# The order of ScalarE's queue, a table for comparisons, and the first tile's softplus on VectorE, in a decoder layer of one core

## The chip, the cores and the metric

One core of a Trainium2 chip runs the whole program. The metric is the device time of one execution in microseconds; the median of three runs is given.

## The reference

A decoder layer on x of shape (4, 512, 512), float32. First a linear attention with 16 heads and decay, worked in chunks of 128 tokens, then an output projection, a residual sum and a layer norm. Then a state space model (selective scan) on a context of (4, 512, 256), gated by the rows of x:

```python
x = silu(xc + conv_b[None, :, None])                       # causal convolution of in_proj(ctx)
x_dbl = jnp.einsum('bdl,ed->bel', x, x_proj_w)
dt_low, Bm, Cm = jnp.split(x_dbl, [dt_rank, dt_rank + d_state], axis=1)
dt = jax.nn.softplus(jnp.einsum('brl,dr->bdl', dt_low, dt_proj_w) + dt_proj_b[None, :, None])
def step(state, inp):                                      # over 512 time steps
    dA = jnp.exp(d[..., None] * A)
    state = state * dA + (d * u)[..., None] * b[:, None, :]
    y = jnp.einsum('bdn,bn->bd', state, c)
y = (y + D[None, :, None] * x) * silu(z)
```

Residual and layer norm again; then a mixture of 64 experts, of which each token takes the 8 with the highest probability (at most 256 tokens an expert), and a last residual and layer norm.

## The kernel before

The program has two parts. `mixers` computes attention, state space model and routing for the four batches; `experts` runs the 64 experts behind it. The change is in `mixers` alone.

`mixers` gives each engine its own queue, written out by hand; semaphores tie them together. All queues follow one pattern: a loop over the batches b, in it the tiles c = 0 to 3 (128 channels of the scan, and at the same time a chunk of 128 tokens of attention, number t = 4b + c), and in it 8 steps k. A step n = 32b + 8c + k works two groups of states: ScalarE makes the decays (`decays`, L856, writes `hst`), GpSimd the inputs (`inputs`, L1120, writes `dbu`; it may run one step ahead), VectorE scans twice and multiplies with C (`scan`, L1301 and L1307), TensorE sums over the states (`sum_states`, L416). Between the steps stands the rest: TensorE's projections (q, k, v at L454, the output at L523), scores (L475), the turning of q and k; ScalarE's copies out of the PSUM ring of three banks (`take`, L831); GpSimd's rotation of q and k (L1193 to L1197), its roots (L1148, L1150) and, in batches 1 to 3, the scattering of the slot table (L1227); VectorE's masks on the scores (L1354), layer norm sums and routing. At tile c = 2 the next batch's convolution is made (`front`), at c = 3 its projections to B, C and the step sizes (`soft`).

The softplus of a tile m of a batch is spread over engines. ScalarE computes |x|, relu(x), exp(-|x|), 1 + it, a rounded copy and the logarithm (`soften`, `exponentials`, `rounded`, `logs`). Then GpSimd and ScalarE work in turn: `soft_parts` (GpSimd, L1126, L1127), `excess` (ScalarE, Relu, L902), `soft_rest` (GpSimd, L1132), `steps` (ScalarE, Relu, L906), `steps_of_u` (GpSimd, L1138, the product with u), which signals `dtu_ready`. SP's queue then copies the result 32 times into `rep` (`copy_steps`, L734), and only then can the decays and inputs of that tile be made. Tiles 0 and 1 are EARLY, tiles 2 and 3 LATE. Batch 0's tile 0 alone is done by VectorE in a row (`first_steps`, L1336 to L1348), before the loop. For tile 0 of batches 1 to 3 the turn is in c = 3 of the batch before: `soft_parts` at k = 4 and `soft_rest` and `steps_of_u` at k = 5 of GpSimd's loop. For tiles 1, 2 and 3 it is in c = 0 and 1 of their own batch. `soft_ready` counts the `soft_rest`s.

In c = 0 ScalarE's queue behind step 5's decays reads: the small copy of ssq, the copy of the k projection, `steps(b, 1)`, `exponentials(b, LATE)`, decays of step 6, and so on; near its end `excess(b, 2)`, decays of step 8, `excess(b, 3)`, the copies of qT and kT.

The routing of the third batch is turned into slots by comparisons: `number_slots` (in the last batch, c = 1, k = 7) computes places, and `make_hots` (L1472) compares them with 0 to 127, twice for each of four chunks of tokens, at the (c, k) of `HOT_AT`. They read `count16`, 128 values of 16 bits, broadcast along the last axis. For the last batch the same is done in the tail behind the loops, with `count8`, in which each value stands 8 times in a row, filled by L1625 in the tail.

## Time and profile before

| | |
|---|---|
| median of 3 runs | 1326.41 us (1325.27 to 1327.13) |
| the profiled execution | 1329.2 us, its span 1327.4 us |
| mean granted TensorE clock | 0.887 of full |
| VectorE busy | 1117.1 us, 84% |
| TensorE busy | 1140.0 us, 86% |
| GpSimd busy | 968.9 us, 73% |
| ScalarE busy | 847.4 us, 64% |

A timeline lists one engine's instructions by start. An idle time ahead of an instruction stands in brackets with the instruction that ended it; without brackets it followed the one before. Instructions in a row of the same line are drawn together (x2). The end of one and the start of the next may overlap by some 0.1 us.

### The profile page before, as it was taken

To read this page: it belongs to the slowest core of one execution; us is meant where nothing else is said; L and a number is where in the kernel's file an instruction comes from. 1 tells how busy PE (TensorE), PEld (TensorE's weight loads), DVE (VectorE), ACT (ScalarE), POOL (GpSimd) and SP (SyncE) were. 2 spreads that over 40 slices of the span, in tenths; PEclk is the share of its full clock that TensorE was granted. 3 is DMA by queue.
4 is the path that set the end of the run, shared out by engine and by line. 5 is a ranking of instruction groups with operands and counts; after the bars stand their busy time and mean duration, and the time that the engine had idled before them with its cause. 6 is when DMAs were issued, how large, how long until landed. Compare 5 with 4: busy or idle time off the path is not lost. (4 is left out here: it accounts for less than half of the span.)

```text
span 1327.4 us, 19360 instructions
## 1 busy us (share of the span) xinstructions
PE 1140.0 (86%) x6421; PEld 759.0 (57%) x6421; DVE 1117.1 (84%) x1564; ACT 847.4 (64%) x1522; POOL 968.9 (73%) x760
## 2 busy tenths in 40 slices
PE   7779998799988989898785659999999999999950
PEld 2334434444433533345332449989999899998940
DVE  3679998889888899888999648988988888888947
...
GB/s 300 80 80 250 89 57 103 143 96 36 66 127 118 74 84 50 136 61 121 69 47 74 100 118 221 306 303 297 301 305 303 305 294 306 301 309 305 285 142 321
DMA packets 95138, 235.03 MB, mean 177 GB/s; under 512 B 18608, under 2 KB 18864, under 8 KB 94400
## 3 DMA queue, kind: packets, MB, share of 16 engines
...
## 5 line engine op out<-in xcount | busy, mean ns | idle before, releaser
L1301 DVE TENSOR_TENSOR_SCAN hst<-hst,dbu 128x512 f32<-128x512 f32 x256 | 299.1, 1214 | 48.4 <-POOL dbu L1120 35.6
L1120 POOL TENSOR_TENSOR dbu<-rep,bc 128x1024 f32<-128x1024 f32 x128 | 301.7, 2361 | 51.7 <-PE y_ps L416 18.5
L1774 POOL DMA_INDIRECT sum_rows<-ye,tokens x128 | 205.3, 1604 | 102.4 <-ACT ye L1850 81.3
L416 PE MATMUL y_ps<-dbu,cs 128*32 128x512 f32 x512 | 161.7, 716 | 73.1 <-DVE dbu L1307 55.3
L856 ACT ACTIVATE hst<-rep,small_sb 128x512 f32<-128x512 f32 x256 | 166.0, 684 | 65.8 <-DVE dbu L1307 61.5
L1766 POOL DMA_INDIRECT xe<-x_rows,tokens x128 | 151.3, 1182 | 74.5 <-issue 37.8
L454 PE MATMUL ring<-first_raw,xT 128*128 128x512 f32 x384 | 176.2, 603 | 2.7 <-ACT made L878 1.9
L1307 DVE TENSOR_TENSOR dbu<-hst,bc 128x1024 f32<-128x1024 f32 x128 | 156.8, 1225 | 4.4
L1816 PE MATMUL low<-xh,w1h 128*128 128x256 f32 x512 | 151.0, 295 | 0.0
L1816 PE MATMUL low<-xl,w1h 128*128 128x256 f32 x512 | 145.7, 285 | 0.0
L1816 PE MATMUL low<-xh,w1l 128*128 128x256 f32 x512 | 145.7, 285 | 0.0
L454 PEld LDWEIGHTS ring<-first_raw,xT 128*128 128x128 f32 x384 | 69.5, 190 | 98.3 <-issue 98.3
L1926 DVE TENSOR_TENSOR w1l<-first_raw,w1h 128x1024 fp32r<-128x1024 f32 (+1 forms) x128 | 117.0, 956 | 9.7 <-ACT w1h L1868 0.7
L1919 DVE TENSOR_TENSOR xl<-turn,xh 128x512 fp32r<-128x512 f32 x128 | 82.7, 687 | 33.1 <-ACT xh L1860 32.4
L1868 ACT ACTIVATE w1h<-first_raw 128x1024 fp32r<-128x1024 f32 (+1 forms) x128 | 101.0, 844 | 5.5 <-PEq L162 5.5
L416 PEld LDWEIGHTS y_ps<-dbu,cs 128*32 128x32 f32 x512 | 20.9, 117 | 138.3 <-DVE dbu L1307 67.0
L1816 PEld LDWEIGHTS low<-xl,w1h 128*128 128x128 f32 x512 | 99.2, 194 | 0.0
L1816 PEld LDWEIGHTS low<-xh,w1h 128*128 128x128 f32 x512 | 99.0, 193 | 0.1
L1816 PEld LDWEIGHTS low<-xh,w1l 128*128 128x128 f32 x512 | 99.0, 193 | 0.0
L475 PEld LDWEIGHTS ring<-qT,kT 32*128 32x128 f32 x512 | 49.2, 280 | 61.0 <-ACT qT L831 28.3
L1804 PE MATMUL turn<-cs,xe 128*128 128x128 f32 x512 | 69.2, 279 | 13.6 <-DMA xe<-x_rows,tokens 12.7
L475 PE MATMUL ring<-qT,kT 32*128 32x128 f32 x512 | 57.3, 388 | 21.1 <-ACT kT L831 21.1
...
## 6 DMA issues: line engine op xcount, KB each, us to landing
first_raw<-in_gate_up SPq DMA_DIRECT2D x64, 768.0 KB, 9.9
rep<-made SPq DMA_DIRECT2D x256, 128.0 KB, 2.4
...
```

Of the source, the lines that this page charges most:

```text
L416: ins = pe.matmul(y_ps[rows, :], sel, dbu[:, n % WORK, g, :], start=(k == 0), stop=(k == QUADS - 1))
L454: ins = pe.matmul(ps[:, :], xT[:, t % 2, k, :], wqkv[:, "qkv".index(name), k, :], start=(k == 0), stop=(k == KD - 1))
L475: ins = pe.matmul(ps[:, g * P:(g + 1) * P], kT[r * HD:(r + 1) * HD, g, :], qT[r * HD:(r + 1) * HD, g, :], start=True, stop=True)
L856: act.activation(hst[:, at % HBANKS, :], rep[:, i % 2, g, 0, :], ACT.Exp, scale=a_sc[:, 4 * m + 2 * half + g, k:k + 1]).then_inc(da_ready, 1)
L1120: pool.tensor_tensor(dbu[:, n % WORK, :, :], rep[:, i % 2, :, 1, :], bc[:, k, 0, :].unsqueeze(1).broadcast_to([P, 2, T]), ALU.mult).then_i ...
L1301: dve.tensor_tensor_scan(h, h, dbu[:, n % WORK, i, :], 0.0, ALU.mult, ALU.add).then_inc(scanned, 1)
L1307: dve.tensor_tensor(dbu[:, n % WORK, :, :], hst[:, first:first + 2, :], bc[:, k, 1, :].unsqueeze(1).broadcast_to([P, 2, T]), ALU.mult).the ...
L1766: pool.indirect_dma_start(xe[:, e % RAW, j, :], None, x2_dram, bass.IndirectOffsetOnAxis(ap=tokens[:, e, j:j + 1], axis=0))\
L1774: pool.indirect_dma_start(sum_dram[e % SUMS], bass.IndirectOffsetOnAxis(ap=tokens[:, e, j:j + 1], axis=0), ye[:, e % YE, j, :], None, comp ...
L1816: ins = pe.matmul(dst, w[:, s, k, at:at + P], x[:, s, k, :], start=(k == 0 and n == 0), stop=(k == KD - 1 and n == 2))
L1868: act.activation(w1h[:, e % 2, :, cols], w1[:, e % RAW, :, cols], ACT.Copy).then_inc(w1h_ready, 1)
L1926: dve.tensor_tensor(w1l[:, e % 2, :, cols], w1[:, e % RAW, :, cols], w1h[:, e % 2, :, cols].bitcast(F32), ALU.subtract).then_inc(w1l_ready, 1)
```

## The change

Three things. On ScalarE, in c = 0, `steps(b, 1)` and `exponentials(b, LATE)` stand ahead of the copy of k, and `excess(b, 3)` behind the copies of qT and kT. The table `count8` lies in a tensor of its own, `counts`, whose first 16 rows hold the weights `dt_wT` until the last use; it is filled in `number_slots` at c = 1 of the last batch, and all comparisons read it (`count16` is gone). And `first_steps` now takes a batch: VectorE does tile 0's last five operations of the softplus in every batch, for batches 1 to 3 behind step 4 of c = 3; GpSimd's four and ScalarE's two operations for it are gone. `soft_ready` counts three a batch now.

```diff
--- before.py
+++ after.py
@@ -173,7 +173,8 @@
         wqkv = first_raw[:, :].rearrange("p (n k d) -> p n k d", n=3, k=KD)
         wo_sb = second_raw[:, 0:KD * D].rearrange("p (k d) -> p k d", k=KD)
         in_wT = second_raw[:, KD * D:].rearrange("p (k n) -> p k n", k=KC)
-        dt_wT = sb("dt_wT", [RANK, INNER])
+        counts = sb("counts", [P, INNER])
+        dt_wT = counts[0:RANK, :]
         small_sb = sb("small_sb", [P, S_END])
         xp_wT = small_sb[:, S_XP:S_R].rearrange("p (m r) -> p m r", m=MI)
         rT = small_sb[:, S_R:S_CONV].rearrange("p (k e) -> p k e", k=KD)
@@ -233,7 +234,6 @@
         tok_i = sb("tok_i", [P, TILES], I32)
         spill_f = sb("spill_f", [P, NT * TOPK])
         chosen = sb("chosen", [P, EXPERTS])
-        count16 = sb("count16", [P, P], F16)
         slot_i = sb("slot_i", [P, 3, NT, TOPK], I32)
         place_of = sb("place_of", [P, 2, NT, TOPK], F16)
@@ -257,7 +257,7 @@
         hot = acc[:, :, :].rearrange("p m t -> p (m t)").bitcast(F16).rearrange("p (i h s k) -> p i h s k", i=2, h=2, k=TOPK)
         hot_last = (bc[:, :, :, :].rearrange("p q a t -> p (q a t)").bitcast(F16)
                     .rearrange("p (j h s k) -> p j h s k", j=NT, h=2, k=TOPK))
-        count8 = xT[:, 0, :, :].rearrange("p k n -> p (k n)").bitcast(F16).rearrange("p (s k) -> p s k", k=TOPK)
+        count8 = counts[:, :].bitcast(F16).rearrange("p (s k) -> p s k", k=TOPK)
         tokens_f = tokens[:, :, :].bitcast(F32)
         tab_i, tab_f = u_sb[:, 2, 0:P].bitcast(I32), u_sb[:, 2, P:2 * P]
@@ -708,7 +708,7 @@
             def load_context(b):
                 if b:
-                    sp.wait_ge(soft_ready, MI * b - 1)
+                    sp.wait_ge(soft_ready, (MI - 1) * b)
                 sp.dma_start(ctxT[:, :, :], ctx_turned[b].rearrange("p (k t) -> p k t", k=KC)).then_inc(ctx_loaded, 16)
             def store_rows(b):
@@ -902,7 +902,7 @@
                 act.activation(ln[m], ln[m], ACT.Relu).then_inc(excess_ready, 1)
             def steps(b, m):
-                act.wait_ge(soft_ready, softened(b, m) - 1)
+                act.wait_ge(soft_ready, (MI - 1) * b + m)
                 act.activation(dt_of(m), dt_of(m), ACT.Relu).then_inc(dt_ready, 1)
             def take_mixed(t):
@@ -1049,27 +1049,24 @@
                         first_tap(b + 1, 2)
                     if soft:
                         rounded(b + 1, 1)
-                        excess(b + 1, 0)
                     if back and c == 1:
                         exponents(b - 1)
                     take_squares(t)
+                    if c == 0:
+                        steps(b, 1)
+                        exponentials(b, LATE)
                     if soft or (back and c == 1):
                         take(f"q{t + 1}", flat(qk[:, 0:HEADS, :]))
                     if more:
                         if c < NT - 1:
                             act.wait_ge(kdec_ready, (NT - 1) * b + c + 1)
                         take(f"k{t + 1}", flat(qk[:, HEADS:, :]))
-                    if c == 0:
-                        steps(b, 1)
-                        exponentials(b, LATE)
                     decays(n + 6)
                     for j in hots_due(n + 6, 2):
                         number_lows(j, hot[:, j % 2, 1, :, :])
                     if front:
                         first_tap(b + 1, 3)
-                    if soft:
-                        steps(b + 1, 0)
                     if c == 0:
                         rounded(b, 2)
                         logs(b, LATE)
@@ -1088,13 +1085,13 @@
                         decays(n + 8)
                         for j in hots_due(n + 8, 2):
                             number_lows(j, hot[:, j % 2, 1, :, :])
-                    if c == 0:
-                        excess(b, 3)
                     if more:
                         if c:
                             act.wait_ge(qdec_ready, (NT - 1) * b + c)
                         take(f"qT{t + 1}", flat(qT[:, :, :]))
                         take(f"kT{t + 1}", flat(kT[:, :, :]))
+                    if c == 0:
+                        excess(b, 3)
             first_norm(NT * B - 1)
             gate_z(B - 1, 3)
             for j in range(NT):
@@ -1266,14 +1263,8 @@
                             gate(b, k - 2)
                         if k == 2 and c == 3 and last:
                             gate(b, 2)
-                        if k == 4 and c == NT - 1 and not last:
-                            soft_parts(b + 1, 0)
-                        if k == 5 and c == NT - 1 and not last:
-                            soft_rest(b + 1, 0)
                         if k == 5:
                             mixed_root(t)
-                        if k == 5 and c == NT - 1 and not last:
-                            steps_of_u(b + 1, 0)
                         if k == (5 if c < NT - 1 else 6) and t + 1 < NT * B:
                             rotate(t + 1)
                         if k in (6, 7) and c == 0:
@@ -1330,22 +1321,23 @@
                     else:
                         ins.then_inc(drain_sem(use), 1)
-            def first_steps():
-                taken(dve, "dt0_0")
-                dve.wait_ge(soft_steps, 2)
+            def first_steps(b):
+                done, tile = 4 * MI * b, softened(b, 0)
+                taken(dve, f"dt{b}_0")
+                dve.wait_ge(soft_steps, done + (3 if b else 2))
                 dve.tensor_tensor(dt_of(0), dt_of(0), acc[:, 0, :], ALU.add).then_inc(part_steps, 1)
-                dve.wait_ge(soft_steps, 4)
-                dve.wait_ge(logged, 1)
+                dve.wait_ge(soft_steps, done + (7 if b else 4))
+                dve.wait_ge(logged, tile)
                 dve.tensor_tensor(ln[0], dtu_of(0), ln[0], ALU.subtract).then_inc(parts_ready, 1)
-                dve.wait_ge(part_steps, 1)
-                dve.wait_ge(parts_ready, 1)
+                dve.wait_ge(part_steps, tile)
+                dve.wait_ge(parts_ready, tile)
                 dve.scalar_tensor_tensor(out=dt_of(0), in0=ln[0], scalar=0.0, in1=dt_of(0), op0=ALU.max, op1=ALU.subtract)\
                     .then_inc(excess_ready, 1)
-                dve.wait_ge(excess_ready, 1)
+                dve.wait_ge(excess_ready, tile)
                 dve.tensor_scalar(dt_of(0), dt_of(0), -1.0, 0.0, ALU.mult, ALU.max).then_inc(dt_ready, 1)
-                dve.wait_ge(dt_ready, 1)
-                dve.wait_ge(u_ready, 1)
-                dve.tensor_tensor(dtu_of(0), dt_of(0), u_of(0, 0), ALU.mult).then_inc(dtu_ready, 1)
+                dve.wait_ge(dt_ready, tile)
+                dve.wait_ge(u_ready, MI * b + 1)
+                dve.tensor_tensor(dtu_of(0), dt_of(0), u_of(b, 0), ALU.mult).then_inc(dtu_ready, 1)
             def mask_scores(t, r):
                 use = f"s{r}_{t}"
@@ -1457,6 +1449,9 @@
                 assert own.n == ROUTE_STEPS, own.n
             def number_slots(b, own):
+                if b == B - 2:
+                    full(dve, f"dt{B - 1}_{MI - 1}")
+                    dve.tensor_copy(count8, cs[:, C_COUNT:C_COUNT + P].unsqueeze(2).broadcast_to([P, P, TOPK]))
                 own.settle()
                 own.step(dve.tensor_scalar(slot_i[:, 0, :, :], idxf[:, 0, :, :], float(P - 1), None, ALU.add))
                 own.settle()
@@ -1467,17 +1462,17 @@
                 dve.tensor_copy(place_of[:, 1, :, :], slot_i[:, 2, :, :]).then_inc(placed, 1)
                 assert own.n == PLACE_STEPS, own.n
-            def make_hots(j, hots, count):
+            def make_hots(j, hots):
                 for h in range(2):
                     ins = dve.tensor_tensor(hots[:, h, :, :], place_of[:, h, j, :].unsqueeze(1).broadcast_to([P, P, TOPK]),
-                                            count, ALU.is_equal)
+                                            count8, ALU.is_equal)
                 ins.then_inc(hots_made, 1)
             def number_tokens(j):
                 dve.wait_ge(placed, 1)
                 if j >= 2:
                     full(dve, f"slots{j - 2}")
-                make_hots(j, hot[:, j % 2], count16[:, :].unsqueeze(2).broadcast_to([P, P, TOPK]))
+                make_hots(j, hot[:, j % 2])
             def add_slots(use, done):
                 ps = full(dve, use)
@@ -1490,7 +1485,7 @@
                 own.settle()
                 dve.wait_ge(placed, 2)
                 for j in range(NT):
-                    make_hots(j, hot_last[:, j], count8)
+                    make_hots(j, hot_last[:, j])
                 taken(dve, "table")
                 ps = full(dve, "slots_last")
                 spares = key[:, 0:2, :].rearrange("p j e -> p (j e)").rearrange("p (e j) -> p e j", j=CJ)
@@ -1513,11 +1508,10 @@
                 convolve(0, m)
             dve.wait_ge(const_loaded, 16)
             dve.memset(ones16[:, :], 1.0)
-            dve.tensor_copy(count16[:, :], cs[:, C_COUNT:C_COUNT + P])
             dve.tensor_copy(below16[:, :], cs[:, C_TRI:C_TRI + P]).then_inc(halves_ready, 1)
             dve.tensor_copy(tok_i[:, :], cs[:, C_TOK:C_TOK + TILES])
             dve.tensor_copy(spill_f[:, :], cs[:, C_TRASH:C_TRASH + NT * TOPK])
-            first_steps()
+            first_steps(0)
             chain = {}
             for b in range(B):
                 last = b == B - 1
@@ -1575,6 +1569,8 @@
                         chain["norm"] = Chain(dve, norm2_steps, NORM2_STEPS * (b - 1))
                         second_sum(b - 1, chain["norm"], 0)
                         second_sum(b - 1, chain["norm"], 1)
+                    if c == NT - 1 and not last:
+                        first_steps(b + 1)
                     if back and c == 1:
                         choose(b - 1, chain["route"])
                     if front:
@@ -1622,7 +1618,6 @@
                 second_sum(B - 1, chain["norm"], j)
                 chain["norm"].settle()
                 dve.bn_aggr(mv2[:, j, :], st2[:, j, :]).then_inc(stats2_ready, 1)
-            dve.tensor_copy(count8, cs[:, C_COUNT:C_COUNT + P].unsqueeze(2).broadcast_to([P, P, TOPK]))
             chain["route"] = shift_logits(B - 1)
             choose(B - 1, chain["route"])
             find_slots(B - 1, chain["route"])
```

ScalarE in tile 0 of batch 0, behind step 5's decays, and at the tile's end (lines of the kernel before; L831 copies out of the ring, L906 is `steps`, L885 and L888 `exponentials`, L856 decays, L902 `excess`):

```order
@@ -47,8 +47,8 @@
 L856 ACTIVATE hst<-rep,small_sb 128x512 x2
 L914 ACTIVATE ssq<-ring0 128x1
-L831 ACTIVATE qk<-ring1 128x512
 L906 ACTIVATE made<-made 128x512
 L885 ACTIVATE acc<-acc 128x512 x2
 L888 ACTIVATE made<-acc,ones 128x512 x2
+L831 ACTIVATE qk<-ring1 128x512
 L856 ACTIVATE hst<-rep,small_sb 128x512 x2
```

```order
 L902 ACTIVATE ctxT<-ctxT 128x512
 L856 ACTIVATE hst<-rep,small_sb 128x512 x2
-L902 ACTIVATE ctxT<-ctxT 128x512
 L831 ACTIVATE qT<-ring1 128x512
 L831 ACTIVATE kT<-ring2 128x512
+L902 ACTIVATE ctxT<-ctxT 128x512
```

The copy of k has moved behind five instructions, and the second `excess` behind the copies of qT and kT.

GpSimd in c = 3 of batch 0, before (L1126, L1127, L1132 and L1138 are the softplus of the next batch's tile 0, L1120 the inputs, L1148 and L1150 the root):

```order
L1120 TENSOR_TENSOR dbu<-rep,bc 128x1024 x3
L1126 TENSOR_TENSOR made<-made,acc 128x512
L1127 TENSOR_TENSOR ctxT<-made,ctxT 128x512
L1120 TENSOR_TENSOR dbu<-rep,bc 128x1024
L1132 TENSOR_TENSOR made<-made,ctxT 128x512
L1148 TENSOR_SCALAR rms<-ssq 128x1
L1150 TENSOR_TENSOR rms<-rms,half_sb 128x1
L1138 TENSOR_TENSOR made<-made,u_sb 128x512
L1120 TENSOR_TENSOR dbu<-rep,bc 128x1024
```

and the same place after the change (its line numbers are three lower):

```order
L1117 TENSOR_TENSOR dbu<-rep,bc 128x1024 x4
L1145 TENSOR_SCALAR rms<-ssq 128x1
L1147 TENSOR_TENSOR rms<-rms,half_sb 128x1
L1117 TENSOR_TENSOR dbu<-rep,bc 128x1024
L1190 TENSOR_TENSOR rot<-qk,cs 128x512 x2
```

The four operations are gone; four input products follow one another.

VectorE after the change, at the same place (L1292 and L1298 are a step, L1328 to L1340 `first_steps`):

```order
L1292 SCALAR_TENSOR_TENSOR hst<-hst,dbu 128x512 x2
L1298 TENSOR_TENSOR dbu<-hst,bc 128x1024
L1328 TENSOR_TENSOR made<-made,acc 128x512
L1331 TENSOR_TENSOR ctxT<-made,ctxT 128x512
L1334 SCALAR_TENSOR_TENSOR made<-ctxT,made 128x512
L1337 TENSOR_SCALAR made<-made 128x512
L1340 TENSOR_TENSOR made<-made,u_sb 128x512
L1292 SCALAR_TENSOR_TENSOR hst<-hst,dbu 128x512 x2
L1298 TENSOR_TENSOR dbu<-hst,bc 128x1024
```

The five stand between step 4 and step 5; before the change the two steps followed each other there.

## Rows read from the trace of the kernel before

**Rows 1.** The page's part 1: busy us (share of the span) xinstructions.

```profile
PE 1140.0 (86%) x6421; PEld 759.0 (57%) x6421; DVE 1117.1 (84%) x1564; ACT 847.4 (64%) x1522; POOL 968.9 (73%) x760
```

**Rows 2.** Timeline of GpSimd: start us, us, engine, line, operation, tiles, count, [idle, releaser].

```profile
780.27 1.07 POOL L1766 DMA_INDIRECT xe<-x_rows,tokens  x1 [28.38 <-POOLq L162]
```

**Rows 3.** Timeline of VectorE, tile 0 of batch 0 and the start of tile 1.

```profile
74.21 2.35 DVE L1301 TENSOR_TENSOR_SCAN hst<-hst,dbu 128x512 f32<-128x512 f32 x2 [3.77 <-ACT hst L856]
...
84.59 2.35 DVE L1301 TENSOR_TENSOR_SCAN hst<-hst,dbu 128x512 f32<-128x512 f32 x2 [1.05 <-POOL dbu L1120]
...
90.81 1.29 DVE L1354 TENSOR_TENSOR pr<-ring,dmask 128x512 f32<-128x512 f32 x2 [1.96 <-PE ring L475]
...
92.02 2.33 DVE L1301 TENSOR_TENSOR_SCAN hst<-hst,dbu 128x512 f32<-128x512 f32 x2
```

**Rows 4.** Timeline of ScalarE, the same stretch.

```profile
70.16 0.60 ACT L831 ACTIVATE qk<-ring 128x512 f32<-128x512 f32 x1 [2.73 <-PE ring L454]
...
73.43 1.29 ACT L856 ACTIVATE hst<-rep,small_sb 128x512 f32<-128x512 f32 x2
...
87.03 0.63 ACT L902 ACTIVATE ctxT<-ctxT 128x512 f32<-128x512 f32 x1 [2.94 <-POOL ctxT L1127]
```

**Rows 5.** Timeline of TensorE, the same stretch: the k and the v projection.

```profile
66.38 3.68 PE L454 MATMUL ring<-first_raw,xT 128*128 128x512 f32 x8
...
75.59 3.70 PE L454 MATMUL ring<-first_raw,xT 128*128 128x512 f32 x8
```

**Rows 6.** Timeline of GpSimd, the same stretch: the product with u.

```profile
71.35 1.27 POOL L1138 TENSOR_TENSOR made<-made,u_sb 128x512 f32<-128x512 f32 x1 [3.31 <-ACT made L906]
```

**Rows 7.** Timelines of ScalarE, GpSimd and VectorE, tile 0 of batch 1.

```profile
231.75 0.60 ACT L831 ACTIVATE qk<-ring 128x512 f32<-128x512 f32 x1 [3.43 <-PE ring L454]
...
235.09 2.49 POOL L1193 TENSOR_TENSOR rot<-qk,cs 128x512 f32<-128x512 f32 x2
...
250.41 2.35 POOL L1120 TENSOR_TENSOR dbu<-rep,bc 128x1024 f32<-128x1024 f32 x1
...
253.61 2.33 DVE L1301 TENSOR_TENSOR_SCAN hst<-hst,dbu 128x512 f32<-128x512 f32 x2
```

**Rows 8.** Timeline of VectorE, second and fifth operation of `first_steps` in batch 0.

```profile
31.65 0.69 DVE L1339 TENSOR_TENSOR ctxT<-made,ctxT 128x512 f32<-128x512 f32 x1 [2.76 <-ACT ctxT L894]
...
33.64 0.69 DVE L1348 TENSOR_TENSOR made<-made,u_sb 128x512 f32<-128x512 f32 x1
```

**Rows 9.** Timelines of VectorE and GpSimd, boundary of batches 1 and 2.

```profile
362.83 2.35 DVE L1301 TENSOR_TENSOR_SCAN hst<-hst,dbu 128x512 f32<-128x512 f32 x2 [1.41 <-ACT hst L856]
...
379.03 2.35 DVE L1301 TENSOR_TENSOR_SCAN hst<-hst,dbu 128x512 f32<-128x512 f32 x2 [3.66 <-POOL dbu L1120]
...
362.73 2.35 POOL L1120 TENSOR_TENSOR dbu<-rep,bc 128x1024 f32<-128x1024 f32 x1
...
367.79 1.27 POOL L1138 TENSOR_TENSOR made<-made,u_sb 128x512 f32<-128x512 f32 x1 [0.54 <-ACT made L906]
```

**Rows 10.** Timelines of VectorE and GpSimd: L1415 beside GpSimd's product and in the tail.

```profile
626.79 3.01 DVE L1415 TENSOR_TENSOR x2T<-x2T,small 128x256 f32<-128x256 f32 x1
...
627.15 2.35 POOL L1120 TENSOR_TENSOR dbu<-rep,bc 128x1024 f32<-128x1024 f32 x1
...
760.77 0.42 DVE L1415 TENSOR_TENSOR x2T<-x2T,small 128x256 f32<-128x256 f32 x1
```

**Rows 11.** Line L1472: count, ns min/median/max; then the first eight with their busy us.

```profile
L1472 DVE TENSOR_TENSOR acc<-place_of,count x8: 1211/1800/5927, 657.7 to 721.4; 128x1024 f16<-128x1024 f16 x8
...
L1472 DVE TENSOR_TENSOR bc<-place_of,xT x8: 683/684/692, 768.0 to 772.2; 128x1024 f16<-128x1024 f16 x8
...
L1472 DVE TENSOR_TENSOR acc<-place_of,count 128x1024 f16<-128x1024 f16 x8 | 19.1, 2421 | 0.0
```

**Rows 12.** Timeline of VectorE in the tail: the table's filling.

```profile
750.18 0.66 DVE L1625 CAST xT<-cs 128x1024 f16<-128x1024 f32 x1
...
758.74 0.42 DVE L1404 TENSOR_REDUCE small<-ring 128x4 f32<-128x256 f32 x1 [7.90 <-PE ring L548]
```

2 lines of the change are left out of this document (1 added, 1 removed).

## The prediction

> **What bounds the kernel now.** I read the busy shares first. TensorE, VectorE and GpSimd are busy for 86, 84 and 73% of the span [rows 1], so the average names no limit and each stretch has to be read by itself. The execution falls in two parts. GpSimd issues the first gather of the experts at 780.27, having waited for the end of the first part (attention and state space model) [rows 2]. The change touches nothing behind that point, so all that is won or lost must be won or lost before it, and passes to the end one to one.
>
> In the first part VectorE runs 128 scan steps. Step n is two scans (2.33 us) and one product, some 3.5 us in all, with other VectorE work between. In the timeline of VectorE most steps start with no idle time before them, so the first part is VectorE's chain with holes, and the reader is to look at the holes in brackets. They stand at the same places in every batch: in tile 0 (chunk 0), at the start of tile 1, and at the first step of the next batch. In batch 0, step 6 waits 3.77 us for ScalarE's decays, step 8 1.05 for GpSimd's product, and the first mask of tile 1 1.96 for the scores of TensorE [rows 3]. The 1.96 before that mask and the 1.05 to 1.10 before step 8 are there in all four batches.
>
> ScalarE's timeline says why. It reaches the copy of the k projection at 67.4 and sits there until 70.16, because TensorE's projection ends only at 66.38 + 3.68 = 70.06; behind it in the queue stand one Relu, two exponentials and two additions (2.8 us), and behind those the decays of step 6 at 73.43 [rows 4, 5]. Later it waits 2.94 us for GpSimd's difference before the last `excess`, and the copies of qT and kT, which the scores need, stand behind that [rows 4]. GpSimd waits too: 3.31 us for the Relu [rows 6].
>
> **Part 1: the order on ScalarE in tile 0.** Nothing is added; three kinds of instruction change place. *Batch 0.* The Relu, exponentials and additions now run from 67.4 to 70.2, in the time that was spent waiting, and end when k is there. The k copy ends at 70.8. The decays of step 6 follow, so their first half is there at 71.4, and the step starts then instead of at 74.21: 2.8 us. GpSimd's product with u moves from 71.35 to 68.1 and the rotation behind it starts at 70.9 with the k copy, so everything behind that on GpSimd comes 2.6 us sooner, which is what steps 7 and 8 wait for. With qT and kT copied ahead of the last `excess` the 1.96 is gone as well. Step 8 starts at 84.59 - 2.6 = 82.0. Its two scans and its product take 3.5 us, the sum of tile 0's output and two masks 1.85, so step 9 starts at 87.35 instead of 92.02: **4.7 us**. What is behind the moved instructions: decays of step 9 now follow `excess`, whose operand is there at about 84.4, so they are ready by 85.7, in time. *Batches 1 to 3.* The same with a tighter bound. In batch 1 the rotation started at 235.09, and it can start behind the k copy at 231.75 + 0.60 = 232.35: 2.7 us [rows 7]. From there GpSimd has no idle time to the input product of step 9 of the batch, at 250.41 + 2.35 = 252.76, so those end at 250.1, and that is where the step starts that started at 253.61: 3.5 us [rows 7]. By the same two differences batch 2 gets 3.6 and batch 3 3.7. Sum of part 1: 4.7 + 3.5 + 3.6 + 3.7 = **15.5 us**. Tile 1 starts with TensorE, ScalarE and GpSimd all waiting for VectorE, so the whole pattern moves as one; TensorE has hardly any idle time in tile 2, but its unbroken run starts from VectorE's events and moves with them. Bounds: nothing beyond the first hole (2.8 + 3 x 1.1 = 6 us), if TensorE's projections hold the rest, and 15.5 + 2.
>
> **Part 2: the softplus of the first tile, at three batch boundaries.** Off GpSimd go four 128x512 operations a boundary (1.27 us each, as the last of them [rows 9], 5.1 us), off ScalarE two Relus; on VectorE come five. Where they stand today, in batch 0 with GpSimd idle, the last four take 33.64 + 0.69 - 31.65 = 2.68 us, and the first, which waited on its own there, is like the second, 0.69: 3.4 us [rows 8]. Take the boundary from batch 1 to 2. VectorE is through with step 4 at 362.83 - 1.41 = 361.4; step 5 starts at 362.83, step 0 of the next batch at 379.03 after a hole of 3.66, since the GpSimd chain gives its result at 367.79 + 1.27 = 369.06 and the copies of SP's queue follow it [rows 9]. Four of the five operations have both inputs in SBUF, and such an operation does not run beside one of GpSimd: with 3.01 us for what takes 0.42 in the tail, L1415 at 626.79 ended at 629.80, just behind the end of GpSimd's product at 627.15 + 2.35 = 629.50 [rows 10]. GpSimd, rid of its softplus work, starts its next product, that of step 6, some 1.9 us before 362.73, where it starts now, when TensorE's sum of step 3 is done, and holds to 363.2 [rows 9]. So the five end at 363.2 + 3.4 = 366.6, with GpSimd's two tiny roots between them 367.1. That is 2.0 us before 369.06, but step 5 now starts 4.3 us late, and steps 5, 6, the attention sum (1.7) and 7 at 3.5 us each put step 0 at 379.3 instead of 379.03: **+0.3**. The same working gives +0.7 at the first boundary and +0.2 at the third: **+1.2 us**. The five operations are hidden by the hole that the old chain left (1.41 + 3.66 us and a small one between), so this trade is nearly even. SP's copies start 2 us sooner, and its row loads behind them; inputs of step 1 of the next batch come 2.3 us sooner on GpSimd. I count none of it, because tile 0 is then held by the k projection, which follows VectorE. Bounds: without any waiting for GpSimd the five end at 364.8 and step 0 starts at 376.9, 2.1 us sooner (4.4 for the three boundaries, by the same working); for the upper end see the second rival.
>
> The Trainium skill ("SBUF — State Buffer", section on SBUF's two separate sides) states that VectorE operations with two SBUF inputs and GpSimd's operations hold one port pair by an exclusive lock, for the whole instruction. The trace agrees, with 3.01 against 0.42 us. By that rule at its worst this part costs what the second rival says; without it this part would give 4.4 us instead of costing 1.2.
>
> **Part 3: the comparisons and their table.** `make_hots` now reads a dense 16-bit table instead of one broadcast along the last axis. Of the eight in batch 3 the shortest took 1.21 us; the eight in the tail, which read such a dense table, 0.68 each [rows 11]. 8 x 0.53 = 4.2 us. The rest of the 19.1 us that they take is waiting for GpSimd: the longest of them lasted 5.93 us, beside two products of GpSimd in a row [rows 11]. I leave that waiting as it is. GpSimd's own small operations stand behind them in the same way, so its chain moves too. **-4.2 us**; ends 0 (the gain goes into new waits for GpSimd) and 19.1 - 4.9 = -14 (no waiting at all, as in the tail). The table's filling, 0.66 us, moves from the tail, where a wait of 7.90 us hides it [rows 12], to the end of tile 1 of batch 3, where VectorE is the chain: **+0.9** with a short wait for GpSimd (0.7 to 3). Removing it from the tail gives nothing. The small cast at the start stood under a wait too.
>
> **Sum.** -15.5 + 1.2 - 4.2 + 0.9 = -17.6. The profiled execution took 1329.2 us (span 1327.4), so it would take 1311.6; the median of the runs stands 2.8 lower, at 1326.4, and would become **1308.8**, say 1309.
>
> **Rivals.** *Half the gain stays behind TensorE* (0.18). The copies of k and v are then paced by TensorE alone. For it: the v projection (75.59 + 3.70) ends at 79.3, and v is taken before the decays of step 8 [rows 5]. Against it: step 8 is at 82.0 in my working, later than that. Part 1 would give 7.7, and the time 1316.6. *The lock turns the sign* (0.04). The place is the five operations at a boundary; if each of the four with two SBUF inputs meets a whole GpSimd product (2.36), a boundary costs 9.4 + 3.4, less the 5.3 of holes, 7.5 us; three are 22.5, and with -15.5 and -3.3 the time is 1330. It decides from 6.3 us a boundary. For it: the longest comparison sat through two products in a row [rows 11]. Against it: GpSimd's next product needs step 5's scan, so it has nothing long to run after 363.2. *The comparisons do not reach the dense rate in the middle* (0.08): no -4.2, 1313. *The comparisons also dodge GpSimd's products*: the 14 us of part 3 in place of 4.2, or half of them, 1299 to 1304 (0.12). The forecast itself has 0.55, with 1304 to 1314; 0.03 is left for no change, if the holes of tile 0 open again elsewhere.
>
> **Numbers.** A measurement of this kernel can tell 0.2%, 2.7 us. Faster 0.93, same 0.03, slower 0.04. The range that holds eight in ten runs from the dodging case to the TensorE case: 1302 to 1318.
>
> **What would show it.** After: no wait of ScalarE ahead of the four operations behind ssq in tile 0, holes before steps 6, 7 and 8 below 1 us and the mask's 1.96 gone; step 9 of batch 0 near 87.4; five VectorE operations in 4.5 to 6 us at each boundary, the first of them long; the hole of 3.66 gone, step 0 of batch 2 about as long after step 4 as before; comparisons in batch 3 with a minimum near 0.68; the first gather near 763. Wrong would be: tile 0 of batches 1 to 3 shorter by under 2 us, or the five operations over 8 us.

## The result and the profile after

| | before | changed |
|---|---|---|
| median beside one another | 1325.84 us (4 runs) | 1306.15 us (4 runs, 1304.74 to 1307.75) |
| ratio | | 0.9864, 95% interval 0.9827 to 0.9901 |
| the profiled execution | 1329.2, span 1327.4 | 1305.6, span 1303.8 |
| VectorE busy | 1117.1 | 1124.0 |
| mean granted TensorE clock | 0.887 | 0.900 |

The forecast was 1308.8, with 1302 to 1318. The changed kernel ran beside the old one twice more, in the experiments: 0.9899 (0.9884 to 0.9914) and 0.9872 (0.9844 to 0.9900). So the gain is 13 to 18 us; the 19.7 us between the two medians in the table are more than any of the three ratios gives.

The page's part 1, beside [rows 1], and the first gather of the experts in GpSimd's timeline, beside [rows 2]:

```profile
PE 1126.6 (86%) x6421; PEld 751.5 (58%) x6421; DVE 1124.0 (86%) x1578; ACT 844.8 (65%) x1516; POOL 954.8 (73%) x748
```

```profile
760.00 1.07 POOL L1761 DMA_INDIRECT xe<-x_rows,tokens  x1 [27.20 <-POOLq L162]
```

VectorE is busy for 7 us more and the program is shorter, because the work went into holes. The gather starts 20.3 us sooner. The experts, which the change leaves alone, took 547.1 us in the profile before and 543.8 here; other profiled executions with the same experts have 542.5 to 547, so this part is chance.

To see where the 20.3 us come from I set scan step against scan step: how much sooner each of the 128 starts than in the profile before.

| at the start of | batch 0 | batch 1 | batch 2 | batch 3 |
|---|---|---|---|---|
| step 0 | 1.6 | 4.7 | 8.7 | 11.9 |
| step 9 | 5.7 | 9.2 | 12.1 | 16.0 |
| step 12 | 4.2 | 6.9 | 11.3 | 15.2 |
| step 4 of c = 3 | 4.7 | 7.4 | 11.3 | 18.9 |
| step 5 of c = 3 (behind the five operations) | 0.3 | 4.7 | 7.0 | 18.8 |

Three things stand in it. Tile 0 gains 4.1, 4.5, 3.4 and 4.1 us by step 9 and gives 0.8 to 2.3 back by step 12. The five operations cost 4.3 us at once (2.7 in batch 1, where a wait of 1.41 had stood, [rows 9]), and all of it is back by the next step 0. Batch 3 gains 3.7 us more behind step 12, from the comparisons. And 1.6 us were there before any scan step. The lead is 18.7 us at step 127 and 20.3 at the gather; the stretch between them gained 0.0 to 1.6 us in every other profile too (1.4 in p1b_excess_only, which has nothing of parts 2 and 3), so these 1.5 us are not put down to any part.

**Tile 0.** VectorE's timeline, tile 0 of batch 0 and the start of tile 1, beside [rows 3]:

```profile
70.37 2.35 DVE L1292 TENSOR_TENSOR_SCAN hst<-hst,dbu 128x512 f32<-128x512 f32 x2 [2.69 <-ACT hst L856]
...
80.93 2.35 DVE L1292 TENSOR_TENSOR_SCAN hst<-hst,dbu 128x512 f32<-128x512 f32 x2 [1.18 <-POOL dbu L1117]
...
85.10 1.28 DVE L1346 TENSOR_TENSOR pr<-ring,dmask 128x512 f32<-128x512 f32 x2
86.30 2.33 DVE L1292 TENSOR_TENSOR_SCAN hst<-hst,dbu 128x512 f32<-128x512 f32 x2
...
97.33 2.35 DVE L1292 TENSOR_TENSOR_SCAN hst<-hst,dbu 128x512 f32<-128x512 f32 x2 [1.40 <-POOL dbu L1117]
```

The masks wait no more, and step 9 starts at 86.30. But step 6 still waits 2.69, and a hole that was not there before has opened at step 11: 1.40, for GpSimd. The timelines of ScalarE and of GpSimd in the same stretch, beside [rows 4, 6]:

```profile
69.09 0.60 ACT L831 ACTIVATE qk<-ring 128x512 f32<-128x512 f32 x1 [1.64 <-PE ring L454]
...
83.37 0.63 ACT L902 ACTIVATE ctxT<-ctxT 128x512 f32<-128x512 f32 x1 [1.20 <-POOL ctxT L1124]
```

```profile
69.82 2.49 POOL L1190 TENSOR_TENSOR rot<-qk,cs 128x512 f32<-128x512 f32 x2 [2.36 <-issue]
...
94.91 4.70 POOL L1117 TENSOR_TENSOR dbu<-rep,bc 128x1024 f32<-128x1024 f32 x2
```

The k copy waits for TensorE's projection as before, with the moved work behind it already done. GpSimd's rotation starts with it, and from there to the input product of step 11, the first of the pair at 94.91, GpSimd is never idle; that product ends at 97.3, where the step starts. When k is there depends on the clock too. The k projection on TensorE, first here, then in the third profile of the changed kernel (after_third), with step 6 in that profile:

```profile
63.61 5.38 PE L454 MATMUL ring<-first_raw,xT 128*128 128x512 f32 x8
```

```profile
67.29 3.68 PE L454 MATMUL ring<-first_raw,xT 128*128 128x512 f32 x8
...
72.43 2.35 DVE L1292 TENSOR_TENSOR_SCAN hst<-hst,dbu 128x512 f32<-128x512 f32 x2 [0.94 <-ACT hst L856]
```

The projection took 5.38 us here, at a mean granted clock of 0.68 of full, and 3.68 before [rows 5] and in after_third. With these instructions ahead of the copy, step 6 waits 2.69 us in all five profiles in which the projection took 5.38, and 0.94 to 1.00 in all four in which it took 3.68.

**The boundary.** Timelines of VectorE and GpSimd, batches 1 and 2, beside [rows 9]:

```profile
353.89 1.76 DVE L1328 TENSOR_TENSOR made<-made,acc 128x512 f32<-128x512 f32 x1
355.57 0.68 DVE L1331 TENSOR_TENSOR ctxT<-made,ctxT 128x512 f32<-128x512 f32 x1
...
357.55 0.69 DVE L1340 TENSOR_TENSOR made<-made,u_sb 128x512 f32<-128x512 f32 x1
358.16 2.34 DVE L1292 TENSOR_TENSOR_SCAN hst<-hst,dbu 128x512 f32<-128x512 f32 x2
...
370.29 2.34 DVE L1292 TENSOR_TENSOR_SCAN hst<-hst,dbu 128x512 f32<-128x512 f32 x2
```

```profile
352.75 2.35 POOL L1117 TENSOR_TENSOR dbu<-rep,bc 128x1024 f32<-128x1024 f32 x1 [1.31 <-DVE hst L1292]
355.67 0.63 POOL L1145 TENSOR_SCALAR rms<-ssq 128x1 f32<-128x1 f32 x1 [0.57 <-ACT ssq L914]
356.39 1.17 POOL L1147 TENSOR_TENSOR rms<-rms,half_sb 128x1 f32<-128x1 f32 x1
```

The first of the five lasts until GpSimd's product is through (352.75 + 2.35 = 355.10); the others run at 0.68 and 0.69 (0.43 for the one with a single input). In all 358.16 - 353.89 = 4.27 us, and 4.34 and 4.35 at the other two boundaries. How long the five take follows what is left of the product when they start: at this boundary the other profiles have 0.27 us left and 3.33 for the five (after_again), 0.97 and 4.03 (after_third), 1.94 and 5.00 (p2_first_tile), and here 1.21 and 4.27, each time 3.06 us more than what was left. GpSimd's tiny roots pay instead: 0.63 and 1.17 us, where they take 0.19 and 0.57 without a neighbour (as at 574.90 further down). Step 0 at 370.29 follows without a hole; the 3.66 is gone.

**The comparisons.** Line L1467 in VectorE's groups (busy, mean ns), beside [rows 11]:

```profile
L1467 DVE TENSOR_TENSOR acc<-place_of,counts 128x1024 f16<-128x1024 f16 x8 | 14.8, 1889 | 0.0
L1467 DVE TENSOR_TENSOR bc<-place_of,counts 128x1024 f16<-128x1024 f16 x8 | 4.9, 685 | 0.1
```

19.1 us have become 14.8, with the waits for GpSimd still in them (the longest is 5.38, the shortest 0.68).

### The profile page after: what moved, and what is told of

Same layout as the page of the kernel before. It is cut to its first block and busy times, and to the rows that moved or that the text cites. A ratio compares the mean times of both kernels' runs of the same rounds, so it can differ in the third digit from the quotient of the medians.

```text
span 1303.8 us, 19359 instructions
## 1 busy us (share of the span) xinstructions
PE 1126.6 (86%) x6421; PEld 751.5 (58%) x6421; DVE 1124.0 (86%) x1578; ACT 844.8 (65%) x1516; POOL 954.8 (73%) x748
## 5 line engine op out<-in xcount | busy, mean ns | idle before, releaser
L1292 DVE TENSOR_TENSOR_SCAN hst<-hst,dbu 128x512 f32<-128x512 f32 x256 | 298.9, 1213 | 30.9 <-POOL dbu L1117 16.2
L416 PE MATMUL y_ps<-dbu,cs 128*32 128x512 f32 x512 | 156.6, 695 | 77.9 <-DVE dbu L1298 54.9
L856 ACT ACTIVATE hst<-rep,small_sb 128x512 f32<-128x512 f32 x256 | 166.1, 684 | 70.5 <-DVE dbu L1298 70.2
L454 PE MATMUL ring<-first_raw,xT 128*128 128x512 f32 x384 | 179.6, 613 | 1.9 <-ACT made L878 1.9
L1298 DVE TENSOR_TENSOR dbu<-hst,bc 128x1024 f32<-128x1024 f32 x128 | 156.7, 1224 | 4.4
L1190 POOL TENSOR_TENSOR rot<-qk,cs 128x512 f32<-128x512 f32 x32 | 40.0, 1271 | 49.6 <-DVE made L1340 32.4
L1224 POOL DMA_INDIRECT slot_table<-tok_i,idx_s x64 | 65.1, 1018 | 13.3 <-issue 11.9
```

Of the source, the lines that this page charges most:

```text
L416: ins = pe.matmul(y_ps[rows, :], sel, dbu[:, n % WORK, g, :], start=(k == 0), stop=(k == QUADS - 1))
L454: ins = pe.matmul(ps[:, :], xT[:, t % 2, k, :], wqkv[:, "qkv".index(name), k, :], start=(k == 0), stop=(k == KD - 1))
L856: act.activation(hst[:, at % HBANKS, :], rep[:, i % 2, g, 0, :], ACT.Exp, scale=a_sc[:, 4 * m + 2 * half + g, k:k + 1]).then_inc(da_ready, 1)
L1292: dve.tensor_tensor_scan(h, h, dbu[:, n % WORK, i, :], 0.0, ALU.mult, ALU.add).then_inc(scanned, 1)
L1298: dve.tensor_tensor(dbu[:, n % WORK, :, :], hst[:, first:first + 2, :], bc[:, k, 1, :].unsqueeze(1).broadcast_to([P, 2, T]), ALU.mult).the ...
```

## The experiments

Each single part was put on the kernel before, or taken out of the changed one. "Rotation" is GpSimd's L1193 (L1190 in the changed kernel), whose start is given behind step 0 of its batch.

### Each part alone, and the changed kernel without part 2

p1_scalar_order is the kernel before with the change's hunks on ScalarE in c = 0 alone.

> Part 1 alone (ScalarE's order in tile 0) on the kernel before. Theory A, GpSimd paces the end: between the two profiles GpSimd's rotation in tile 0 of batch 0 came 3.7 us sooner and everything behind it on GpSimd came as much sooner without idle time, so VectorE, which was 5.7 us ahead at step 9, was 4.2 ahead behind step 11; over the four tiles 3.0 + 2.4 + 2.5 + 3.3 = 11.2 us, so about 1315 us. Theory B, the working of the forecast: 15.5 us, so about 1310. If the gain of the two profiles needs the other parts (GpSimd without the softplus of the boundary), it is under 9 us, above 1317.

Measured: 1315.28 beside 1323.89, ratio 0.992 (0.9897 to 0.9944), some 10.6 us. Theory A holds; the forecast's 15.5 lies outside the interval (7.4 to 13.6 us).

p2_first_tile is the kernel before with `first_steps(b + 1)` and without GpSimd's and ScalarE's operations for it.

> Part 2 alone (the first tile's softplus on VectorE in every batch). Theory A: as the profile of the changed kernel shows, the five operations take 4.3 us and not 5.7, and the old hole of 3.7 pays for them: a boundary gains 0.1 to 1.3 us, 2.0 in all, so about 1324. Theory B, the forecast's working: costs 1.2 us, 1327. A third: the inputs of the next tile 0 come sooner on GpSimd, and without part 1 the wait for the k projection eats that: no difference at all, 1326.

Measured: 1326.56, ratio 1.0011 (0.9991 to 1.0032). Alone the part gains nothing. The third guess fits: in batches 2 and 3 step 4 stood 2.0 us sooner behind step 0 than before, and step 6 no sooner (31.8 and 32.2 us, against 32.0). ScalarE's old order stands in the way there, as its timeline in batch 2 shows:

```profile
405.50 0.60 ACT L831 ACTIVATE qk<-ring 128x512 f32<-128x512 f32 x1 [3.43 <-PE ring L454]
405.99 0.62 ACT L906 ACTIVATE made<-made 128x512 f32<-128x512 f32 x1
```

p3_counts is the kernel before with the table `counts` alone.

> Part 3 alone (the dense table for the comparisons). Both theories: eight comparisons at 0.53 us less each, 4.2 us, and 0.6 to 0.9 us for the filling, so 3.4 us less, about 1322.5; the shortest comparison near 0.68 us, the longest still over 5 us. A rival: the first 1.6 us of the changed kernel's lead, which it had before any scan step, belong to the new place of the table (then step 0 starts at about 42.1 here too, and the time is 1321); if they are chance, step 0 starts at 43.7 or 42.1 with no connection to the part.

Measured: 1322.86, ratio 0.998 (0.9959 to 1.0002), so the time alone says little. The steps say it: between the start of c = 2 and the end of c = 3 of batch 3 the lead over the profile before grows by 4.3 us, in four pieces of some 1.1, after 0.6 had been lost to the filling (0.78 us in the changed kernel's timeline, at 632.80). The groups of VectorE:

```profile
L1476 DVE TENSOR_TENSOR acc<-place_of,counts 128x1024 f16<-128x1024 f16 x8 | 14.8, 1888 | 0.0
```

Step 0 started at 42.2 here and in p2_first_tile, at 44.6 in p1_scalar_order and at 44.1 in p13. In after_again, which is the changed kernel, it was 44.3, so the 1.6 us at the start are chance and belong to no part.

p13_no_first_tile is the changed kernel with part 2 undone:

```diff
-                    if c == NT - 1 and not last:
-                        first_steps(b + 1)
...
+                        if k == 4 and c == NT - 1 and not last:
+                            soft_parts(b + 1, 0)
+                        if k == 5 and c == NT - 1 and not last:
+                            soft_rest(b + 1, 0)
```

> The changed kernel without part 2. If the parts add up, part 1 and part 3 give 11.2 + 3.5, about 1311 us, and part 2 is worth the remaining 4 to 5 us to 1306, more than the 2 us that the two profiles show at the boundaries. If part 2 is a trade that costs (the forecast's working), this kernel is faster than the changed one, about 1305.

Measured: 1311.2, ratio 0.9891 (0.9871 to 0.9911). It ran once more, beside the changed kernel.

> The changed kernel without part 2, beside the changed kernel. The first call gave it 0.9891 of before, the changed kernel 0.9864 and 0.9899. Theory A, part 2 is worth 2 to 3 us behind part 1 (step 4 of tile 0 in batches 2 and 3 at 17.7 us behind step 0 and not 19.5, and in batch 3 the rotation at 28 and not 30): this one is 2 to 3 us above the changed kernel. Theory B, it is an even trade here as it was alone (1.0011, 0.9991 to 1.0032): equal within 1 us.

> The changed kernel, the partner of the one without part 2. 0.9864 to 0.9899 of before, so 1306 to 1310. TensorE's granted clock sets about 1 us a batch in it: tile 0 lasts 39.5 us where the stretch's mean clock is 0.87 and 40.7 where it is 0.83, and this run shows either.

Measured: 1311.58, ratio 0.9901 (0.9876 to 0.9925), against 1309.43, ratio 0.9872 (0.9844 to 0.9900). The intervals overlap, so the 2.2 us are not shown by this pair; all 12 runs without part 2 have a median of 1311.3, all 14 of the changed kernel 1308.1, but most of these did not run side by side. The traces agree with theory A, and show the place. Batch 3 without part 2 (p13_no_first_tile), first VectorE, then GpSimd:

```profile
565.25 2.35 DVE L1301 TENSOR_TENSOR_SCAN hst<-hst,dbu 128x512 f32<-128x512 f32 x2 [1.71 <-POOL dbu L1120]
```

```profile
573.54 1.27 POOL L1138 TENSOR_TENSOR made<-made,u_sb 128x512 f32<-128x512 f32 x1
574.90 0.19 POOL L1148 TENSOR_SCALAR rms<-ssq 128x1 f32<-128x1 f32 x1
575.17 0.57 POOL L1150 TENSOR_TENSOR rms<-rms,half_sb 128x1 f32<-128x1 f32 x1
575.72 2.47 POOL L1193 TENSOR_TENSOR rot<-qk,cs 128x512 f32<-128x512 f32 x2
```

and in the changed kernel GpSimd at the same place:

```profile
570.54 2.49 POOL L1190 TENSOR_TENSOR rot<-qk,cs 128x512 f32<-128x512 f32 x2 [0.36 <-ACT qk L831]
```

Without part 2 GpSimd comes to the rotation late and without idle time, 30.0 us behind step 0 (575.72 - 545.75); with it GpSimd is there before k, at 27.8 (570.54 - 542.72). Not all of these 2.2 us are GpSimd's: k was copied by 28.6 without part 2 and by 27.7 with it. Beyond k, GpSimd was 1.3 us late, and 1.8 in p13_again. In the second profile of the changed kernel (after_again) k came late as well and the rotation stood at 29.0, so there only 0.8 to 1.0 us of batch 3 are left. Part 2 had made the next batch's first inputs sooner (the second product of the pair starts 2.0 us ahead of step 0, at 368.33 against 370.29; before it was 0.65 behind, 379.68 against 379.03), and so much of this lead is kept in batch 3, where ScalarE no longer holds it up.

### The halves of part 1

```diff
                     take_squares(t)
+                    if c == 0:
+                        steps(b, 1)
+                        exponentials(b, LATE)
```

(and gone behind the copy of k) is p1a_steps_only; p1b_excess_only is the other half:

```diff
-                    if c == 0:
-                        excess(b, 3)
                     if more:
...
                         take(f"kT{t + 1}", flat(kT[:, :, :]))
+                    if c == 0:
+                        excess(b, 3)
```

> Of part 1 only steps(b, 1) and exponentials(b, LATE) ahead of the copy of k, on the kernel before. Theory A, part 1's gain is the shift of GpSimd's rotation (from 31.2-31.6 us behind step 0 to 27.8-29 in batches 1 to 3), and what VectorE has more by step 9 it gives back at step 11: this half alone moves the rotation as much, so it gives nearly all of part 1, 8 to 9 us, 1315; the wait of 1.96 us ahead of the first mask stays or shrinks, and the hole before step 11 is gone or smaller. Theory B, the forecast's addition: without the 1.96 of the mask in each batch it gives 15.5 less 7.8, near 8 too, but then the other half alone gives the rest.

> Of part 1 only excess(b, 3) behind the copies of qT and kT, on the kernel before. Theory A: the 1.96 us ahead of the first mask of tile 1 is gone in all four batches, and comes back at step 11 or 12, since GpSimd's rotation stays at 29.8 to 31.6 us behind step 0; in batch 0 step 11's inputs are done at 100.9 and the step started at 101.6, so 0.7 us at most, and 0 to 2 us in all. Theory B, the forecast's addition: 4 x 1.96, near 7 us.

Measured: 1315.62, ratio 0.993 (0.9910 to 0.9950), some 9 us, and 1323.41, ratio 0.9986 (0.9967 to 1.0005), some 2 us; theory A in both. The second half removed the wait of 1.96 in all batches; in batch 0 VectorE had 2.0 us more at step 9, and then

```profile
101.70 2.35 DVE L1301 TENSOR_TENSOR_SCAN hst<-hst,dbu 128x512 f32<-128x512 f32 x2 [1.39 <-POOL dbu L1120]
```

gave 1.4 of it back at step 11. The reason stands in this table: start of the rotation behind step 0, start of step 11 behind step 0, and the difference, from the timelines of each profile (batch 0 / 1 / 2 / 3).

| | rotation | step 11 | difference |
|---|---|---|---|
| before | 29.8 / 31.6 / 31.2 / 31.2 | 57.9 / 60.9 / 60.5 / 61.8 | 28.1 / 29.3 / 29.3 / 30.6 |
| p1b | 28.9 / 30.4 / 31.1 / 31.6 | 56.4 / 59.7 / 60.5 / 62.2 | 27.5 / 29.3 / 29.4 / 30.6 |
| p1a | 27.7 / 28.8 / 29.0 / 30.2 | 55.8 / 58.1 / 58.3 / 60.9 | 28.1 / 29.3 / 29.3 / 30.7 |
| p1 | 27.7 / 27.8 / 28.8 / 30.0 | 55.2 / 57.1 / 58.2 / 60.7 | 27.5 / 29.3 / 29.4 / 30.7 |
| p13 (first) | 27.2 / 27.8 / 29.0 / 30.0 | 54.7 / 57.2 / 58.3 / 60.6 | 27.5 / 29.4 / 29.3 / 30.6 |
| changed | 27.7 / 27.8 / 28.6 / 27.8 | 55.2 / 57.2 / 58.0 / 58.5 | 27.5 / 29.4 / 29.4 / 30.7 |

In a given batch the difference is the same to 0.1 us in every kernel of the table, and in p2_first_tile, p3_counts and the later profiles of the changed kernel, except in batch 0 without the second half (28.1, VectorE's own pace; 27.5 is GpSimd's). Wherever GpSimd sets it, the input product of step 11 ends 0.03 us ahead of the step. Step 11 is set by the rotation and GpSimd's unbroken work behind it. Whatever VectorE wins beyond that is waiting.

### What the five operations wait for

```diff
                     first = (2 * n) % HBANKS
+                    if between is not None:
+                        first_steps(between)
                     dve.tensor_tensor(dbu[:, n % WORK, :, :], hst[:, first:first + 2, :],
```

in `scan`, called with `b + 1` for step 4 of c = 3; the old call is gone.

> The changed kernel once more, beside the others of this call. All theories: about 18 us below the kernel before, 1306. If part 2 is worth 5 us behind parts 1 and 3 (this kernel against the one without part 2, 1311), its scan step 4 in the first tile of batches 2 and 3 stands 17.7 us behind step 0, and not 19.5. The lead of 1.6 us that it had at step 0 comes and goes by chance (single parts showed -1.6, -1.5, +0.4 and +0.9): step 0 between 42 and 45 us.

> The changed kernel with the five VectorE operations of a boundary between step 4's scans and its product, so that they start together with GpSimd's input product, which waits for the same scan. Theory A, an operation of VectorE with both inputs in SBUF waits for GpSimd's running product: the first of the five, 1.8 us now, takes 2.3 + 0.7 = 3.0 us, the other four stay at 0.7 and 0.4, each boundary is 1.2 us longer, 3.6 in all, so 1310. Theory B, the first is long for another reason (it follows a product whose input lies in PSUM): it is at 0.7 or stays at 1.8, and the time is that of the changed kernel or less.

Measured: the changed kernel 1309.19, ratio 0.9899 (0.9884 to 0.9914); between_scans 1311.23, ratio 0.9923 (0.9909 to 0.9936), 2 us more, with intervals that just touch; the traces are clearer. The five took 5.37, 5.39 and 5.16 us a boundary, 0.8 to 1.1 us more each. VectorE's timeline at the boundaries of batches 0 and 1 and of 1 and 2:

```profile
180.61 0.69 DVE L1330 TENSOR_TENSOR made<-made,acc 128x512 f32<-128x512 f32 x1
181.22 2.85 DVE L1333 TENSOR_TENSOR ctxT<-made,ctxT 128x512 f32<-128x512 f32 x1
...
352.34 2.89 DVE L1330 TENSOR_TENSOR made<-made,acc 128x512 f32<-128x512 f32 x1
```

and GpSimd's:

```profile
180.68 2.84 POOL L1117 TENSOR_TENSOR dbu<-rep,bc 128x1024 f32<-128x1024 f32 x1 [2.20 <-DVE hst L1292]
...
352.33 2.35 POOL L1117 TENSOR_TENSOR dbu<-rep,bc 128x1024 f32<-128x1024 f32 x1 [1.30 <-DVE hst L1292]
```

At 352.3 both start together, GpSimd has the way first, and VectorE's 0.69 becomes 2.89. At 180.6 VectorE is 0.07 ahead: its first operation takes 0.69, GpSimd's product is 0.5 longer, and it is the *second* operation that sits through it. So theory A holds but for a detail: the wait goes to the operation that meets a running product, whichever of the five it is (the third, 2.65 us, at the third boundary). Theory B falls: in the first and third boundary the first operation was not long at all, though it followed a scan out of PSUM. The Trainium skill ("SBUF — State Buffer", section on SBUF's two separate sides) says that whichever engine's operation starts first has the ports for its whole instruction, and the other is blocked. By that rule VectorE's operation at 352.34 ends 0.69 us behind the end of the product (352.33 + 2.35), which is 3.03 us, and GpSimd's product at 180.68 ends 2.35 behind 181.30, which is 2.97; with 2.89 and 2.84 the trace agrees to 0.15 us.

### Two tries to go further

i12_rotation_later:

```diff
                         exponentials(b, LATE)
+                        decays(n + 6)
...
-                        if k == (5 if c < NT - 1 else 6) and t + 1 < NT * B:
+                        if k == (5 if 0 < c < NT - 1 else 6) and t + 1 < NT * B:
                             rotate(t + 1)
```

(`decays(n + 6)` behind the copy of k only where c is not 0).

> A try to beat the changed kernel: in tile 0 of each batch ScalarE makes step 6's decays ahead of the copy of k, and GpSimd makes the inputs of step 7 ahead of the rotation, which waits for k. Theory A, in batch 0 GpSimd's chain from k on paces step 11: the wait of 2.4 us ahead of the rotation is filled by the inputs, so batch 0 gains up to 2.4 us (not over the hole of 1.4 before step 11 plus what VectorE had ahead), batches 1 to 3, where the wait is 0.4 to 0.7, as little; about 1303. Theory B, the k projection and what TensorE does behind it pace tile 1, not GpSimd: no difference, 1306.

Measured: 1314.53, ratio 0.9947 (0.9934 to 0.9961), 5 us slower than the changed kernel beside it (1309.19); neither theory had that. GpSimd in batch 0:

```profile
70.05 2.36 POOL L1119 TENSOR_TENSOR dbu<-rep,bc 128x1024 f32<-128x1024 f32 x1 [2.66 <-ACT qk L831]
72.35 2.49 POOL L1192 TENSOR_TENSOR rot<-qk,cs 128x512 f32<-128x512 f32 x2
```

The inputs of step 7 did not fill the wait of 2.4 us; they waited 2.66 themselves and pushed the rotation from 69.82 to 72.35 (27.7 to 30.3 us behind step 0, and to 31.8 to 32.4 in the other batches). `inputs(n + 7)` may not start before TensorE has summed step 4 (its buffer is one of three), and that sum is queued behind the k projection: it runs from 68.85 to 69.90; the profile names ScalarE's copy, which ends at about the same time. Step 6, which the earlier decays had brought forward by 2.3 us, had given it all back by step 8. From the rotation to step 11 it is now 25.2, 27.0, 27.0 and 28.4 us, in each batch 2.3 less than in the table: the one product that now stands ahead of the rotation. So the path behind the rotation is the same, and its start came 2.6 us later in batch 0 than in the first profile of the changed kernel and 3.1 to 4.6 in the others; less the 2.3, this accounts for step 11 being 0.3 to 2.3 us late in each batch.

i3_logits_later:

```diff
-                    if back and c == 1:
-                        chain["route"] = shift_logits(b - 1)
...
                     if back and c == 1:
+                        chain["route"] = shift_logits(b - 1)
                         choose(b - 1, chain["route"])
```

> A try to beat the changed kernel: VectorE takes the router's logits behind scan step 4 of tile 1 and not behind step 3, where it waits 4.7, 3.2 and 1.8 us for TensorE in batches 1 to 3 (3.1, 3.2 and 1.8 in the kernel before, so 1.5 us of part 1's gain in batch 1 ends there). If that wait only stands in VectorE's way, 3.5 us of scan fill it: 3.5 + 3.2 + 1.8, less a new wait of 0.5 for ScalarE's exponentials in each, about 7 us, 1299. If TensorE itself is the bound of tile 1 (it takes the q and k projections, 7.1 us, right behind the logits), or the ring's bank is held longer, the holes come back at steps 5 and 6: no difference.

Measured: 1307.25, ratio 0.9889 (0.9873 to 0.9904): no difference from 0.9899 that can be told. The changed kernel waits here, in batch 1 (it was 3.13 in the profile before):

```profile
264.26 0.42 DVE L1396 TENSOR_REDUCE small<-ring 128x4 f32<-128x256 f32 x1 [4.71 <-PE ring L548]
```

In i3 this wait is gone and step 12 starts 61.8 us behind step 0 in place of 66.3 (65.9 in after_again). At the start of c = 2 the lead of batch 1 over after_again, measured from step 0, is gone. In VectorE's and TensorE's timelines of i3:

```profile
268.65 2.04 DVE L1407 TENSOR_TENSOR x2T<-x2T,small 128x256 f32<-128x256 f32 x1
```

```profile
267.65 1.02 PE L514 MATMUL ring<-ones,rot 128*128 128x1 f32 x8 [0.37 <-DVE x2T L1398]
268.53 7.11 PE L454 MATMUL ring<-first_raw,xT 128*128 128x512 f32 x16
```

A routing operation with two SBUF inputs now meets GpSimd (2.04 us against 0.42), TensorE waits for the bank that the logits hold, and its q and k projections start 268.53 - 201.27 = 67.3 us behind step 0, no sooner than in the changed kernel, where they start at 266.18 - 198.78 = 67.4. That TensorE, and not VectorE, paces this stretch fits these rows; which of the three costs most was not separated.

### What the clock is worth

The changed kernel ran with three profiles. Windows over tile 0 of batch 1 (us, busy of PE, PEld, DVE, ACT, POOL, then granted clock), in the first and in after_again:

```profile
198.80:238.30 39.50, 36.70 (x174) 16.64 (x176) 38.53 (x47) 28.17 (x44) 34.71 (x27) 0.87 0.42 99
```

```profile
200.90:241.60 40.70, 38.17 (x174) 17.88 (x176) 38.66 (x46) 28.16 (x44) 33.80 (x27) 0.83 0.39 93
```

The same instructions take 1.2 us longer at the lower mean clock, and the k copy starts 28.2 us behind step 0 and not 27.1. The k projection itself takes 3.68 us in both; it starts 24.5 us behind step 0 and not 23.3. In the three profiles of the changed kernel the copy lies between these two in batches 1 to 3, from batch to batch and from execution to execution. Tile 0 lasts 39.5 us in five of these nine cases, at mean clocks of 0.87 to 0.91, and 40.7 in two, at 0.83; but the other two are 40.35 at 0.87 and 39.99 at 0.83. So the mean clock goes with the time without fixing it, and that it is a good part of why one execution of this kernel differs from the next by some us fits these rows, but is not shown.

## Why the prediction was right, and where not

**The sum** was -17.6; the three ratios of the changed kernel give 18.0, 13.4 and 17.0. By the working its terms were off in both directions: part 1 was put 4.9 us too high and part 2 some 3 to 4 too low. That the sum came out so near is in part luck.

**Part 1** was sized at 15.5 and is worth 10.6 (7.4 to 13.6). The mechanism was right: the two waits of ScalarE cover the moved work and the mask's wait is gone. By step 9 the profile of part 1 alone had 4.2, 4.6, 3.1 and 1.9 us, 13.8 of the 15.5 (forecast 4.7, 3.5, 3.6 and 3.7), and the changed kernel, with part 2's help in batch 3, 4.1, 4.5, 3.4 and 4.1. The step that failed is "so the whole pattern moves as one": I counted the gain at step 9 and let it pass to the end. In tile 1 GpSimd is 27.5 to 30.7 us behind its own rotation whatever VectorE does, so the gain is the rotation's shift: with part 1 alone 2.1, 3.8, 2.4 and 1.2 us, and step 11 moved by 2.7, 3.8, 2.4 and 1.1, 10.0 in sum (in the changed kernel 2.1, 3.8, 2.6 and 3.4, and 2.7, 3.7, 2.5 and 3.3). Two smaller things follow and cancel: the wait for the router's logits in batch 1 grew from 3.13 to 4.71 (in the other profiles of the changed kernel it is that of batch 2 or 3 that grew), and the wait of 1.41 before step 5 at the end of that batch [rows 9] was gone (it stands in batch 2 of p1a_steps_only, so it may move by chance). The rival "half the gain stays behind TensorE" had the right kind of answer, with the wrong stretch.

**Part 2** was costed at +1.2. Alone it is +1.5 (-1.2 to +4.2). In the changed kernel's profile the three boundaries, from step 4 to the next step 0, gained 0.0, 1.3 and 0.6 us, but of the 1.3 at the second the kernel without part 2 had as much (its lead grew from 6.1 to 7.8 there). Behind part 1 the part is worth 2 to 3 us by traces and medians. Two terms were off. The five took 4.3 us and not 5.7: GpSimd's product began 1.1 us before VectorE was through with step 4 (352.75 and 353.89), so that 1.2 us of it were left, where I had it last to 363.2 against 361.4, 1.8 us; and the tiny roots, for which I had added 0.5, did not hold VectorE, VectorE held them. And "I count none of it" was wrong together with part 1: the 2 us by which step 4 comes sooner in batches 2 and 3 survive in part where ScalarE's order no longer holds step 6 up: in batch 3 the rotation came at 27.8, 29.0 and 27.8 us in the three profiles of the changed kernel, against 30.0 and 29.8 without part 2, and in batch 2 at 28.6, 27.8 and 28.3, against 29.0 and 28.8. That is 0.2 to 2.2 us a batch, a part of it k's own.

**Part 3** went as worked out: 0.53 us a comparison, 4.2 to 4.3 us in all, the waiting for GpSimd untouched (5.38 us the longest), the filling 0.6 to 0.8.

**The rivals.** The lock did not turn the sign, since it never meets more than one product: one operation of five a boundary, even where they were put at the worst place. The comparisons reached the dense rate and did not dodge GpSimd. Of the listed signs, step 9 of batch 0 (86.3, with 1.6 of chance in it, against 87.4), the vanished holes and the minimum of 0.68 are there; the hole before step 6 stayed at 2.69 in the first profile, not below 1, since the k projection took 5.38 us at a lower clock where I had its 3.68 of before, and since VectorE reached step 6 1.1 us sooner (its wait before step 4 is 0.73 and was 1.82; this wait comes and goes between 0.57 and 1.83 whatever the kernel). In after_third the hole is 0.94, as forecast, so this sign failed by the clock and by where VectorE stood, and not by the mechanism; the five needed less than the 4.5 us I gave as their least. The first gather at 760.0 was 3 sooner than forecast, of which 1.6 is the start and 1.5 the stretch behind step 127.
